# Waiting for the stores at the end of a program on GpSimd instead of SyncE

## The reference

```python
y = einsum('bct,bcd->bdt', x, weights[conditions])      # 32 x 32 x 256
h = silu(einsum('bsh,hi->bsi', y, w_gate)) * einsum('bsh,hi->bsi', y, w_up)
h = h with the two largest magnitudes of each group of 4 kept, the others 0
out = x + einsum('bsi,ih->bsh', h, w_down)
```

## Time and profile before

| | |
|---|---|
| time, median of 3 executions | 80.19 us |
| lowest and highest | 80.17 and 80.28 us |
| the profiled execution | 80.31 us |
| span of its trace | 78.4 us |
| PE busy | 73.9 us (94%) |
| POOL busy | 8.1 us (10%) |

### The profile page before, as it was taken

How to read it: one execution, slowest core, us unless ns; L and a number is a source line. 1 busy time by engine, 2 the same in 40 slices (tenths; PEclk the granted TensorE clock), 3 DMA queues, 4 the chain that set the end, 5 groups by cost and what they waited for, 6 DMA issues and landing times.

```text
span 78.4 us, 1027 instructions
## 1 busy us (share of the span) xinstructions
PE 73.9 (94%) x362; PEld 59.6 (76%) x362; DVE 62.7 (80%) x93; ACT 42.1 (54%) x62; POOL 8.1 (10%) x17
## 2 busy tenths in 40 slices
PE   3988999999999999999999999999999999999950
PEld 1328888888888888888888888888888888888840
DVE  1006884689889999599999979999999999994460
ACT  6122773799443465699897769798380402720000
POOL 3460000000000013000804000006200000000000
PEclk9999999999999999999999999999999999999999
DMA  0726979995910005900199990003994000003333
GB/s 1 273 95 168 286 234 318 302 418 180 410 67 0 0 0 98 169 0 0 36 196 199 184 192 8 4 0 67 201 180 88 0 0 0 8 0 140 135 134 126
DMA packets 4565, 9.64 MB, mean 123 GB/s; under 512 B 560, under 2 KB 2864, under 8 KB 4304
## 3 DMA queue, kind: packets, MB, share of 16 engines
q1 hardware_dynamic: 3488, 6.16, 23.0%
q0 software_dynamic: 928, 3.28, 21.9%
q10 hardware_dynamic: 144, 0.13, 0.5%
HBM read 5.38 MB, written 1.05 MB: 82 GB/s over the span
## 4 chain that ended last, share of the span: by engine, by line
PE 94%; issue 1%; DVE 1%
PE banks L579 52%; PE banks L621 28%; PE banks L541 6%; PE banks L564 4%; PE banks L591 3%; PE banks L550 1%; DVE gate_raw L455 1%; DVE warm L458 0%
## 5 line engine op out<-in xcount | busy, mean ns | idle before, releaser
L579 PE MATMUL banks<-y_hl,up_hl 128*128 128x512 f32 x96 | 24.2, 389 | 0.0
L621 PE MATMUL banks<-h_hl,down_hl 128*128 128x512 f32 (+1 forms) x102 | 22.0, 376 | 0.0
L579 PE MATMUL banks<-y_hl,gate_hl 128*128 128x512 f32 x84 | 21.4, 390 | 0.0
L621 PEld LDWEIGHTS banks<-h_hl,down_hl 128*128 128x128 f32 x102 | 18.5, 188 | 3.6
L579 PEld LDWEIGHTS banks<-y_hl,up_hl 128*128 128x128 f32 x96 | 18.0, 188 | 3.8
L579 PEld LDWEIGHTS banks<-y_hl,gate_hl 128*128 128x128 f32 x84 | 15.7, 188 | 3.2
L264 ACT ACTIVATE silu<-banks 128x512 f32<-128x512 f32 x16 | 9.6, 597 | 11.1 <-PE banks L579 10.8
L404 DVE TENSOR_TENSOR h<-banks,silu 128x512 f32<-128x512 f32 x12 | 8.2, 687 | 3.8 <-ACT silu L264 3.7
L285 ACT ACTIVATE h_hl<-h 128x1024 fp32r<-128x1024 f32 (+1 forms) x8 | 6.7, 842 | 3.9 <-DVE h L440 3.9
L440 DVE SCALAR_TENSOR_TENSOR h<-count,h 128x512 f32<-128x512 bf16 x12 | 7.9, 685 | 0.1
L271 ACT ACTIVATE x_sb<-h 128x512 f32<-128x512 f32 x8 | 4.9, 625 | 1.7 <-DVE h L404 1.7
(11 more groups left out here) (39 smaller groups left out, 66.7 us busy)
## 6 DMA issues: line engine op xcount, KB each, us to landing
h_hl<-h POOLq DMA_DIRECT2D x4, 512.0 KB, 6.1
x_sb<-in_x SPq DMA_DIRECT2D x2, 512.0 KB, 3.7
up_raw<-in_w_up SPq DMA_DIRECT2D x4, 256.0 KB, 4.3
down_raw<-in_w_down SPq DMA_DIRECT2D x1, 1024.0 KB, 7.6
gate_raw<-in_x_t SPq DMA_DIRECT2D x1, 1024.0 KB, 5.9
down_hl<-down_raw POOLq DMA_DIRECT2D x2, 512.0 KB, 4.9
gate_raw<-in_w_gate SPq DMA_DIRECT2D x3, 256.0 KB, 4.1
out<-gate_raw SPq DMA_DIRECT2D x3, 256.0 KB, 2.3
```

The costliest lines, as they stand in the source:

```text
L579: last = nc.tensor.matmul(dst, w_hl[w][:, s, q, k, j], y_hl[:, m, half, k], start=i == 0, stop=i == len(terms) - 1)
L621: last = nc.tensor.matmul(bank[:, begin:end], down_hl[:, s, q, j, k * P:(k + 1) * P], h_hl[:, u, m, j, begin:end], start=(q, j, m, s) == f ...
```

## The change

SP no longer waits for `stored` at the end of its program. POOL, which had nothing more to do after its last transfer, waits for it at the end of its own program. The value waited for is the same.

```diff
@@ @block.sync
                     sp.wait_ge(out_done, i + 1)
                     sp.dma_start(out[:, k, cols], xt_sb[:, k, cols]).then_inc(stored, 16)
-            sp.wait_ge(stored, 16 * (len(OUTPUTS) - 1))
 
         @block.gpsimd
...
@@ @block.gpsimd
             for u in range(SENT):
                 for j, end in PARTS[u]:
                     low_h(u, j, end)
+
+            pool.wait_ge(stored, 16 * (len(OUTPUTS) - 1))
```

## The result

The change makes the kernel slower: 81.00 us median against 80.19 us, over 7 runs of each, a ratio of 1.0087 with a 95% interval of 1.0062 to 1.0111. The forecast was 80.25 us, in a range of 80.08 to 80.63 us; the time lies above it. The profiled execution took 81.15 us with a span of 79.3 us, against 80.31 us and 78.4 us, so what lies around the span is the same, 1.9 us (it is 1.75 to 1.9 us in all seven executions of the changed kernel).

The account below looks back on a forecast made before the run. The path from the last store's landing to the end was taken as bound: 78.05 + 0.15 + 0.05 + 0.04 = 78.29 us for POOL's first semaphore instruction, against 78.23 before. Adding 0.06 us to 80.19 gave 80.25 us, range 80.08 to 80.63 us.

Parts of the forecast that it names:

- SP's side: End of SP's program: jump and addition to `gather` done by 76.7 us, under the last store's flight, costing nothing.
- The jump, 0.15 us: POOL's jump after its wait for the stores: 0.15 us to its drain, taken from SP's row; bounds 0.04 and 0.20 us.
- the step, 0.04 us: At the end barrier, from the end of POOL's drain to its first semaphore instruction: 0.04 us, read at the start.
- the rival of the fetched instructions: POOL's jump at the end stalls for an instruction fetch: up to 1.4 us added, 81.6 us; chance 0.03.
- The drain with nothing left to do: POOL's drain at the end barrier, after the landing: 0.05 us, from 0.01 up to 0.4 us.
- POOL's drain still owes for its transfers: POOL's end drain does 0.4 us of work for its earlier transfers even when reached 18 us later: 80.6 us; chance 0.36.
- the forecast's 0.53: Chance given to POOL's end drain staying below 0.15 us, with the time within 0.2% of before.
- The price that only a rule gave: POOL's end drain at the skill's constant of some 12 ns: sum 0.04 us smaller, an estimate of 80.21 us.

Follow-up runs that it names:

- the first experiment: The changed kernel with one more POOL drain ahead of POOL's wait for the stores; 80.34 us, ratio 0.9989 to the kernel before the change.
- the kernel with two transfers behind its last one: The changed kernel with a POOL drain added after the first unit's two adding transfers, leaving two of eight for the last drain; 80.46 us, one execution.

## Why the prediction was wrong

**The shape was right.** The landing did not move against the issue of the store (1.9 us after it, as before), SP's side was covered (its drain at 76.64 us, where I had it at about 76.6 us), nothing was queued behind POOL's wait but its part of the barrier, and this part came onto the path.

**The jump, 0.15 us, and the step, 0.04 us, were right.** POOL's jump to its drain measured 0.16 us (78.17 to 78.33 us); from the drain's end (78.33 + 0.71 = 79.04 us) to the semaphore instruction it is 0.05 us. With 0.16 us, where it asked for up to 1.4 us more, the rival of the fetched instructions fell.

**The drain was mis-sized.** This is the step that failed: "The drain with nothing left to do". I took 0.05 us, from the start barrier, and gave 0.4 us as the upper bound. It measured 0.712 us. The 0.05 us itself is right for a drain that has no transfer behind it: 47 ns in the first experiment. But POOL's drain at the end has eight transfers behind it, and the drain at the start, from which I read the value, had none. The rival "POOL's drain still owes for its transfers" named the mechanism and had 0.36, less than the forecast's 0.53, because I held it against it that POOL had 17 us to settle. It does not use them: the runs show 83 ns for each transfer, paid by the next drain, 11 to 18 us after the last landing. The size of that rival was wrong too: 80.6 us, and with it the upper end of the range, 80.63 us, lie below the 81.00 us measured.

**The bound was no bound.** I read 0.4 us off the stretch between the last landing and the end of the drain before, and took it for the whole of what a drain behind transfers owes. What is owed for all eight is 665 ns on top of the 47. That drain had run for 5.8 us ahead of the last landing, so it may have dealt with a part before; but not in the simple way that only the last transfer is left, since 47 + 83 ns would be 0.13 us. The drain in the middle, from the kernel with two transfers behind its last one, has six behind it and ends 0.3 us after the last landing (issued at 42.20 us, landed 6.4 us later):

```profile
L248 POOLq DRAIN  x1: 6750/6750/6750, 42.2 to 42.2; - x1
```

By the trace's own marks of the landings the stretch is 0.38 us with eight transfers and 0.30 us with six. It grows with their number too, and two values don't tell how. What a drain does while a transfer is still in flight stays open. With 0.71 us in place of 0.05 us, the same sum gives 80.25 + 0.66 = 80.91 us, where 81.00 us was measured.

**The price that only a rule gave** was further off. The Trainium skill's constant of some 12 ns for the drains around the program, on all five engines ("VectorE: DVE Perf Modes", section "The DRAIN you can't avoid"), holds for none of POOL's rows here: 47 ns with nothing behind it, 712 ns with eight transfers. The measurement decides. That section speaks of the drains that the runtime puts before and after a program, and those of L48 and L685 belong to the program's own barriers, so it may not be meant for them, and I should not have applied it. SP's drain of 123 ns right behind the issue of a store differs from its 7 ns at other places as well.

## What to carry to other kernels

An engine that looks free may have unpaid work: what a moved wait pushes behind itself on its new engine is part of its price, even if it is only a drain that has always been hidden. If POOL has issued transfers and its last drain would come late, drain it early, under other work; here that bought back the whole 0.7 us. And try the wait for the last store behind the barrier at the block's end, on SP: here that gave 79.3 us instead of 80.3 us, the best of all the kernels tried.

## What the runs showed of the hardware

A drain on POOL, once its transfers had landed, took 47 ns plus 83 ns for each transfer that POOL had issued since its last drain (0, 2, 8 and 16 of them: 47, 213, 712 and 1370 ns), whatever their size (2 KB or 512 KB each) and whether the last had landed 11 or 18 us before. With a transfer still in flight the drain lasted until 0.3 to 0.4 us after its landing. SP's drain, behind 18 transfers that SP had issued and that had landed, took 7 ns. A jump that waits for a semaphore was followed by the next instruction 0.15 us after its start on SP, 0.16 us on POOL and 0.21 us on DVE (77.95 to 78.16 us, in stretches 10 ns wide). And with the last wait behind the barrier, the time outside the span fell from 1.9 us to 1.3 to 1.4 us when SP was the engine that still waited, to some 1.5 us with ACT, and not at all with POOL; what runs in that time is not shown.
